# Moving the DMAs of the row maxima from SyncE's queue to ScalarE's, one unit behind the copy that feeds them

## The reference

```python
scores = jnp.einsum('bhqd,bhkd->bhqk', q, k) / math.sqrt(HD)
scores = scores + mask[None]
attn = jax.nn.softmax(scores, axis=-1)
out = jnp.einsum('bhqk,bhkd->bhqd', attn, v)
```

## Time and profile before

| what | value |
|---|---|
| median of 3 runs | 2834.61 us (2833.82 to 2835.52) |
| profiled execution, its own time | 2834.0 us |
| its span in the profile | 2832.2 us |
| busy: PE, DVE, ACT, POOL | 2383.4, 1830.1, 1364.2, 512.9 us |
| stream of L0, first to last exponential | about 101 to 1380 us |
| stream of L3 | about 2384 to 2667 us |
| DMA_DIRECT2D of the rows of maxima | 240, all issued by SP |

### The profile page before, as it was taken

How to read it: one execution, slowest core, us unless ns; L and a number is a source line. 1 busy time by engine, 2 the same in 40 slices (tenths; PEclk the granted TensorE clock), 3 DMA queues, 4 the chain that set the end, 5 groups by cost and what they waited for, 6 DMA issues and landing times. The chain is left out here.

```text
span 2832.2 us, 37728 instructions
## 1 busy us (share of the span) xinstructions
PE 2383.4 (84%) x12692; PEld 999.5 (35%) x12692; DVE 1830.1 (65%) x4370; ACT 1364.2 (48%) x2333; POOL 512.9 (18%) x603
## 2 busy tenths in 40 slices
PE   6799999999999999999678798984556987999638
PEld 4333334343434434333243323431122533333215
DVE  3686777777776777777237765358999145877242
ACT  2365666666666666666535123344222612566420
POOL 1211111110111111010014001006896002100000
PEclk7799999999999999999889898986899986999868
DMA  2221222221222222121010000003332012222020
GB/s 91 83 90 43 81 66 69 74 82 53 70 65 79 69 66 81 50 71 54 20 36 1 22 1 27 0 12 120 126 138 100 23 44 69 83 64 74 20 90 15
DMA packets 77451, 171.60 MB, mean 61 GB/s; under 512 B 23049, under 2 KB 38665, under 8 KB 73163
## 3 DMA queue, kind: packets, MB, share of 16 engines
q1 hardware_dynamic: 77258, 169.18, 18.8%
HBM read 128.41 MB, written 39.71 MB: 59 GB/s over the span
## 5 line engine op out<-in xcount | busy, mean ns | idle before, releaser
L1056 ACT ACTIVATE sb_prob<-ps 128x512 f32<-128x512 f32 (+1 forms) x1520 | 805.3, 575 | 483.4 <-PE ps L846 307.9
L820 PE MATMUL ps<-sb_k_stack_half,sb_q_stack_half 78*128 78x512 bf16 (+3 forms) x1920 | 588.1, 340 | 56.2 <-DMA sb_q_stack_half<-q_rows 24.5
L846 PE MATMUL ps<-sb_q_stack_half,sb_k_stack_half 81*128 81x128 bf16 (+2 forms) x2240 | 569.8, 312 | 53.4 <-ACT sb_prob L1056 51.9
L957 DVE TENSOR_REDUCE sb_row_max<-ps 128x1 f32<-128x512 f32 x640 | 431.7, 686 | 140.6 <-PE ps L820 138.8
L966 DVE CUSTOM_DVE_ANT_0 sb_masked_scores<-ps,sb_mask_row,sb_row_max 128x128 bf16<-128x128 f32 (+3 forms) x640 | 341.2, 544 | 93.3 <-PE ps L820 90.0
L966 DVE CUSTOM_DVE_ANT_0 sb_masked_scores<-ps,sb_mask_row 128x128 bf16<-128x128 f32 (+3 forms) x640 | 283.2, 487 | 172.1 <-PE ps L820 171.3
L846 PEld LDWEIGHTS ps<-sb_q_stack_half,sb_k_stack_half 81*128 81x128 bf16 x2240 | 201.8, 99 | 385.6 <-ACT sb_prob L1056 199.2
L867 PE MATMUL ps<-sb_prob,sb_v_first_half 128*9 128x512 f32 (+3 forms) x2560 | 300.3, 542 | 0.2 <-ACT sb_o_raw L1063 0.2
L820 PEld LDWEIGHTS ps<-sb_k_stack_half,sb_q_stack_half 78*128 78x128 bf16 x1920 | 184.4, 100 | 268.7 <-DVE sb_row_max L966 79.4
L2606 PE MATMUL ps<-sb_read_out,sb_ident 128*128 128x512 f32 x256 | 139.6, 678 | 119.7 <-DVE sb_read_out L2693 113.8
L2660 POOL TENSOR_TENSOR sb_inflow<-sb_delta_u,sb_b_spread 128x1024 f32<-128x1024 f32 x64 | 201.4, 3162 | 26.3 <-DVE sb_states L2682 19.0
(11 more groups left out here) (375 smaller groups left out, 3171.6 us busy)
## 6 DMA issues: line engine op xcount, KB each, us to landing
sb_q_stack_half<-q_rows SPq DMA_DIRECT2D x240, 96.0 KB
sb_k_stack_half<-k_rows SPq DMA_DIRECT2D x40, 576.0 KB
o_rows<-sb_o_raw SPq DMA_DIRECT2D x80, 256.0 KB, 2.3
sb_b_spread<-b_rows SPq DMA_DIRECT2D x32, 512.0 KB, 4.7
sb_c_spread<-c_rows SPq DMA_DIRECT2D x32, 512.0 KB, 3.5
sb_k_stack_half<-k_rows SPq DMA_DIRECT2D x40, 288.0 KB
q_rows<-sb_qk_parts SPq DMA_DIRECT2D x60, 128.0 KB, 2.1
k_rows<-sb_qk_parts SPq DMA_DIRECT2D x60, 128.0 KB, 2.1
```

The lines of the kernel that those rows point to most:

```text
L820: pe.matmul(M.ps[:, k % RING, 0:hi - lo], qst[half][0:S1_ROWS, s, j, at:at + P], kst[half][0:S1_ROWS, s, lo // CH, j, 0:hi - lo], start=Tr ...
L846: mm = pe.matmul(bank[:, x * w + lo:x * w + hi], kst[half][0:S2_ROWS, s, t // 4, j, t % 4 * P:(t % 4 + 1) * P], qst[half][0:S2_ROWS, s, j, ...
L957: dve.reduce_max(rowmax[:, tau % 3, 0, at:at + 1], M.ps[:, k % RING, 0:w], AX_X).then_inc(first_done, 1)
L1056: act.activation(prob[:, st % PROB_STEPS, heads[0]:heads[-1] + 1, a:CH], scores.rearrange("p (j q) -> p j q", j=len(heads)), ACT.Exp).then ...
```

## The change

SP no longer has the duty "rows". ScalarE issues the three DMAs of a turn itself: in its list of units it keeps the last turn in `late`, and issues after the unit that follows the turn. Where the step is one of the first steps, which have no task, it issues at once. The semaphore counts, the DMAs and their sizes are as before. The wait on `unit_done` is kept, now on ScalarE, for its own copy.

```diff
         for tau in range(self.NT):
             l, b, half, g = self.tasks[tau]
-            duty.setdefault(self.turn_step[tau] + 1, []).append((0, "rows", tau))
             saved = self.last_core
@@ block.sync
-                def max_rows(tau):
-                    l, b, half, g = tasks[tau]
-                    s = plan.slot[tau]
-                    sp.wait_ge(unit_done, plan.turn_unit[tau] + 1)
-                    for part in range(3):
-                        row = S1_ROWS + part
-                        sp.dma_start(qst[half][row:row + 1, s, :, :].rearrange("o j (i q) -> o (j i) q", i=4),
-                                     turned[ROWS * part:ROWS * (part + 1), tau % 2, :]).then_inc(rows_in[half][s], 16)
-
@@ block.scalar
+                def max_rows(tau):
+                    half, s = tasks[tau][2], plan.slot[tau]
+                    act.wait_ge(unit_done, plan.turn_unit[tau] + 1)
+                    for part in range(3):
+                        row = S1_ROWS + part
+                        act.dma_start(qst[half][row:row + 1, s, :, :].rearrange("o j (i q) -> o (j i) q", i=4),
+                                      turned[ROWS * part:ROWS * (part + 1), tau % 2, :]).then_inc(rows_in[half][s], 16)
+
...
-                before = None
+                before, late = None, None
                 for s, step in enumerate(steps):
                     for x, (kind, tau, heads, _) in enumerate(step["units"]):
                         if kind == "turn":
                             turn(step["units_at"] + x, tau)
                         else:
                             weight(step["units_at"] + x, tau, step["t"], heads)
+                        if late is not None:
+                            max_rows(late)
+                        late = tau if kind == "turn" else None
+                        if late is not None and step["task"] is None:
+                            max_rows(late)
+                            late = None
                         if x == 0:
                             for done in plan.saves.get(s, ()):
                                 save(done)
```

More of the change, by code:

```diff
@@ L791, in _ @@
                     for _, what, x in plan.duties[s]:
-                        if what == "rows":
-                            max_rows(x)
-                        elif what == "out":
+                        if what == "out":
                             o_rows(x)
```

## The result

| | before | changed |
|---|---|---|
| median of 6 runs each, us | 2834.22 (2828.11 to 2835.52) | 2866.46 (2855.38 to 2883.62) |
| ratio, 95% interval | 1 | 1.0121 [1.0086, 1.0156] |
| profiled execution: time, span | 2834.0, 2832.2 | 2883.62, 2881.8 |
| granted clock, mean of the span | 0.906 | 0.896 |
| PE busy, us | 2383.4 | 2418.1 |

The change makes the kernel 1.2% slower, 32 us. Its six runs spread over 28 us, those of the kernel before over 7; in the largest later group, 23 runs of the kernel before spread over 30 us, so the spread says little. The profiled execution happens to be the slowest of the six, so its own 49.6 us are more than the typical loss. I read it for mechanisms, and take sizes also from a second profile of the same kernel, further down, at 2854.3 us.

The account below looks back on a forecast made before the run. PE was taken to bound the kernel. To the profiled 2834.0 us came 17 us of PE waits and 5 us of lower clock, with 0 for SP's relief: forecast 2856.6 us, 0.8% slower, range 2838 to 2892.

Parts of the forecast that it names:

- my own case: Slower: ScalarE's hold behind each turn makes PE wait, plus a lower clock; 2842 to 2869 us, chance 0.56.
- SP's relief is 0: SP's 240 freed issues and earlier stacks gain PE nothing; taken as 0, bounds 0 and -5.6 us.
- rival 3: SP was the hidden bound: earlier stacks end 5.6 us of waits in L3; -7 us, 2827.6, faster; chance 0.06.
- The hold: ScalarE's next item starts no earlier than 1.85 us after the start of the unit behind the turn.
- Rival 1: ScalarE is held longer, by DMAs starting behind the exponential or waiting for SP's issues; middle 2881 us; chance 0.22.
- The walked places: Four turns of L0's stream followed with ScalarE delayed: costs to PE 0, 0, 1.2 and 0.8 us, 2.0 a period.
- End of a task: Two exponentials at a task's end: the second ends late and PE's matmul moves, costing 0.8 us.
- The second GELU kind: Around the other kind of GELU place, among the four other turns of a period: under 0.03 us each.
- The sum of 17 us: PE's added waits: 12.4 us in six periods of L0's stream, 4.8 in the 32 other turns.
- The clock behind the GELU: After longer PE waits the granted clock falls, 1.3 us at each of seven places; 0 to 9 us, taken as 5.
- The steepness in the hold: PE's cost rises steeply with ScalarE's hold: 5.4 us at 1.2, 17 at 1.85, 37 at 2.45, 65 at 3.0.
- rival 2: No change: ScalarE's hold is short (1.2 us) or absorbed, costing 0 to 5 us, 2835 to 2840; chance 0.16.

Follow-up runs that it names:

- the hold alone on the chip: Against the kernel before: SP keeps issuing the rows, and ScalarE issues three more DMAs of the same size into a spare on-chip tile; 2867.52 us, ratio 1.0108.
- Two kernels with holds of 1.15 and 1.3 us: The change with two issues behind the first unit, one behind the second: 2864.59 us; the kernel before plus three ScalarE DMAs from a constant tile to DRAM: 2859.5 us.
- The kernel that spreads only the two places: The changed kernel, with the three issues spread over three units only in turns of tasks 1 and 4 of each eight; 2849.51 us, again 2852.72 us.
- the kernel that spreads all turns: The changed kernel, with one of the three issues behind each of the three units after every turn; 2839.78 us, ratio 1.0008.

## Why the prediction was right, and where its sizes were off

The forecast was 2856.6 us, slower; the change measured 2866.46 and, again, 2861.54. Both lie in the range, and the sign and mechanism are those of my own case. The wait and the clock are both in the loss, but the clock has more of it than I gave it. By its steps:

- **PE bounds, SP's relief is 0.** Right, to within 0.8 us. Its direct test is the hold alone on the chip, which keeps all of SP's work and costs 1.0108, against 1.0121 and 1.0093 for the change. PE's waits for stacks stayed at 23.7 us. They also kept the two in L3 that rival 3 wanted gone: 4.8 us, against 5.6 in the earlier trace rows.
- **The hold: 1.85 us from the start of the exponential.** Right to 0.01 (756.03 to 757.88). The issue is 608 ns where I took 589, with full overlap. Rival 1, a longer hold through a late start or through SP's issues, is not seen: over the 80 turns the three issues take 1.80 us at the median, though single turns reach 2.96 in one profile and 3.07 in the other. No overlap with an exponential, one of my bounds, was tried as a kernel: 2894.3, where I had put 2881.
- **The walked places.** PE's wait at the GELU: 4.25, foretold 4.1 (the walk itself moved the exponential by 1.31 and booked 1.2; the wait grew by 1.35). End of a task: a wait of 0.66 and a cost of 0.7, foretold 0.8. The place of the earlier trace rows cost 0. The place of the earlier trace rows was the tight one, with a margin of 0.1 us, and held. The second GELU kind, which I had at under 0.03, costs up to 0.9 and sometimes gains 0.4. The sum of 17 us for the waits stands: in L0's stream alone PE's idle time grew by 15.3 and 18.0 us, and its waits for exponentials in both streams from 51.9 to 67.4.
- **The clock behind the GELU** is the term that was mis-sized. "I take half, 5." Half was a choice between bounds, and that it came near is luck: 3 of 6 places in the first profile, 1 of 6 in the second. But I had priced a fall as 0.22 of 6 us from the earlier trace rows, 1.3 us, and it costs 2.5 to 3.1: the rate is already down when PE restarts (its first matmul takes 0.61 us where it took 0.39), and is not back after the 6 us that I looked at alone. And the places that do not read 0.50 read 0.66 to 0.69 in the first profile and not 0.72, at some 0.4 us each, a term that I had at zero. In L0's stream PE was busy for 15.6 and 7.9 us more, against the 5 us of the forecast for the whole.
- **The steepness in the hold** was wrong in its place. I had the walk fall from 17 us at 1.85 to 5 at 1.2. Two kernels with holds of 1.15 and 1.3 us cost 29 and 22 us. The walk counts how long PE waits, and there it holds: PE stood still 8.4 and 7.5 us longer in L0's stream. The rest is the lower clock, which these two kernels met in four and in six of six places, with a wait longer by 0.7 and 0.8 us. The chance of rival 2 (a short issue, 5 us) rested on this step: a hold of 1.2 us would not have saved the time.
- **The period** grew from 163.9 by 3.1 to 7.7 us over the two profiles (foretold 2 to 3).

Of the loss in a profile, the streams account for 35.2 of 49.6 us in the first and 28.7 of 20.2 in the second. The rest, +14.4 and -8.5, stands ahead of, between and behind the streams, where next to no DMA was moved, and differs between runs of one kernel. That both medians came within 10 us of the forecast is in part luck for this reason too.

"Perfetto Trace Analysis" of the Trainium skill, section on the HWDGE DMA instruction, has a sequencer stay held until the descriptors are made. By that rule ScalarE cannot start its next instruction during an issue, and the trace agrees: ScalarE is idle for 1.25 us ahead of the exponential behind three issues. "DMA: Bandwidth & Descriptors", section "Issuing engines are not separate DMA queues", would have a second issuer save the first one's issue time and no more; the runs agree: with SP's 1.82 us a turn saved or kept the ratio is the same within its interval (1.0121 and 1.0093 against 1.0108).

**What stays open.** The kernel that spreads only the two places costs 17 us in two separate measurements, and the kernel that spreads all turns costs 2.5, not measurable. Both have PE's wait at 2.98 us there. The profiles of the first happen to be of its shortest runs, and show 3.3 and 5.2 us in the streams. That its longer runs lose the rest to the clock is supported by the correlation of time and clock, and not shown, since no profile is of such a run. Nor is it shown what sets the moment at which the clock falls, on which it hangs whether a place stands at 0.50, nor how the share of such places goes with the length of the wait. A single DMA for all 48 rows, which would hold ScalarE for one issue, and issues by POOL were not tried.

## What to carry to other kernels

Count a DMA issue as an instruction on the engine that issues it, in the place where it stands, and read its length from a row of its own kind: 0.44 to 0.63 us on ScalarE here, and half the bytes were no cheaper. Under a longer instruction the first is free and those behind it are not, so spread them, or leave them with an engine that nobody waits for. Where PE stands still for some microseconds in every period, price a longer wait with the clock behind it, which here cost about twice the added wait where a place stood at 0.50, and take several runs, since that was so in some periods and not in others. A changed timing ahead of such a wait can cost the same with the wait as it was. A lead over the reader is slack only as long as no duty that waits is put ahead.

## What the runs showed of the hardware that I had not expected

- An issue's length does not follow its bytes: 608 ns (median) for 16 rows of 128, 627 ns for 8 rows of 128. It follows its kind: 438 ns where the same 16x128 go from a tile to DRAM, 608 ns where they go into a tile on the chip. And it follows its place in the row: of three in a row in the changed kernel the first takes 511 ns at the median, the others 608 and 611.
- The issue starts beside a running exponential of the same engine (756.03 and 756.04 us) and holds only what comes next (at 757.88).
- The granted clock behind one and the same wait of 4.25 us is 0.50 in some periods and 0.69 in others of one execution, and behind one of 2.90 us it is 0.72 in one kernel and 0.50 in five of six periods of another.
- The two kernels with the rows later on SP each had one run far outside, 4556 us and 5281 us, at a mean granted clock of 1.0, which the ratios leave out; no other kernel had one, and why is open.
